# A post-norm attention and FP4 feed-forward layer on one core: a new order of work on four engines, a seeded value bias, a 17-matmul down projection

## The chip, the core and the metric

The kernel runs on one core of a Trainium2 chip. A core has TensorE (matmuls, PE in the profile; its weight loads are PEld), VectorE (DVE), ScalarE (ACT), GpSimd (POOL) and the SyncE queue (SP), each with its own program in order; they meet through semaphores. The metric is the device time of one execution in microseconds, the median of three runs.

## The reference, cut to what matters

The input is 16 sequences of 512 tokens of width 256. A linear attention with softmax features is followed by a residual and a layer norm, and then by a gated feed-forward layer (FFN) of hidden width 704 whose inputs and weights are rounded to FP4 in blocks of 16, again with residual and norm.

```python
q = features(x @ Wq + bq); k = features(x @ Wk + bk); v = x @ Wv + bv   # softmax over each head's 16
context = (q k^T / (sum(q) + eps)) v                                    # no softmax over tokens
x = layernorm(x + context @ Wo + bo)
gate = fp4(x) @ fp4(w_gate).T;  up = fp4(x) @ fp4(w_up).T
h = silu(gate) * up
x = layernorm(x + fp4(h) @ fp4(w_down).T)
```

## The kernel before

**Tiles and steps.** The 8192 tokens are NT = 64 tiles of 128 tokens, NS = 16 sequences of T = 4 tiles. `run` writes out, on every engine, a list of steps; step m of the attention works on tile m, and on older tiles with fixed lags. The FFN has steps of its own, 68 later (`JOIN = NS + 1` sequences), so that its tile 0 is begun in step 68; its preparations begin eight steps earlier. Nothing is scheduled at run time: the order written is the order run.

**Precision.** Every large product is made of three float32r products of a high and a low part (`three`, L859 in the profile): x_hi w_hi, x_hi w_lo, x_lo w_hi, for each of its chunks of 128 rows. ScalarE makes the high part (an `ACT.Copy`), VectorE or GpSimd the low part (a subtraction).

**An attention step on TensorE**: query and key (`pqk`, 6 matmuls of 512 columns), which add onto a bias that ScalarE has put into the bank (`seed`, L471); the value (`pv`): one matmul of `ones_r` with `bias_r` (L907) that opens the bank with the value bias in two pieces, then 6 of 256 columns; for tile m-2 the transposes of its features (L927) and the key-value sums (L929); the output projection of tile m-7 (`out_step`, 6 of 256 columns). Once in four steps there are the product of the sequence's sums with Wo (`pc`, L916), which needs VectorE's `kv_m`, and two transposes of one piece of FFN weights (L899). VectorE takes the maxima (L698), subtracts (L723), sums (L713) and inverts (L729), ScalarE takes the exponential (L533) and copies, GpSimd multiplies (`feat`, L374).

**The FFN weights** are 18 pieces of 128 rows (`NW`), one piece per sequence of attention steps, quantised by a chain over GpSimd, ScalarE and VectorE that ends with transposes, `wf_hi` (ScalarE, L548) and `wf_lo` (VectorE, L742). Pieces 17 and 18 fall into FFN steps 0 and 4; TensorE waits for the last one at FFN step 4.

**An FFN step on TensorE**: `gate_up(0)` (12 matmuls of 352 columns), transposes of the quantised hidden values of tile m-3 (`hq`, L970) and of the input of tile m+1 (L977), the down projection of tile m-4 (`three` over IC = 6 chunks: 18 matmuls of 256 columns), `gate_up(1)`. ScalarE runs Silu on the first half of tile m (L585) and the second half of tile m-1 (L571), the two steps of the rounding (L605, L610) and the high parts (L589, L594); VectorE multiplies (L824, L784), finds block maxima (L834, L793), inverts (L815) and makes low parts (L829, L840); GpSimd scales (`hxn`, L431), adds (`hc`, L416) and rescales (`hq`, L436). The last chunk of the hidden width holds 64 rows of data and 64 of zeros.

**Layer norms** take their statistics from ScalarE (`squares`, L492) and do 13 dependent small operations on VectorE (`layer_norm`, L641 to L655) for a batch of tiles at once. `LN_A` and `LN_B` give each batch's first tile, count, operations per step and first step; for the attention 24 and then 40 tiles, the second batch from attention step 72 on (FFN step 4).

## Time and profile before

| what | us |
|---|---|
| median of 3 runs | 745.06 (744.97 to 745.64) |
| the profiled execution's own time | 742.99 |
| its span, from the first to the last instruction | 741.3 |
| TensorE busy in the span | 705.2 |
| first attention tile's query and key until the last tile's | 8.28 to 252.95 |
| first `gate_up(0)` until the last tile's | 272.10 to 710.23 |

A row of a timeline gives the start and the length of an instruction, or of several merged, and in brackets how long the engine had been idle and what released it. Two successive starts give what an instruction costs when the engine is saturated; its length is longer, since matmuls overlap. A row of groups gives count, busy time, mean length, and idle time ahead of it. Windows give for each engine the busy time in a stretch and the mean granted clock as a share of 2.4 GHz.

### The profile page before, as it was taken

The page shows a single profiled execution, that of the slowest core. Times are in us where ns is not written, and L with a number is a line of the kernel's source. Part 1 is how long each engine was busy: PE and PEld are TensorE (multiplying, and loading weights), DVE is VectorE, ACT ScalarE, POOL GpSimd, SP SyncE. Part 2 cuts the span into 40 slices and gives each one's busy share as a digit, 9 for nine tenths or more (in the row PEclk, how much of TensorE's full clock was granted, in tenths as well). Part 3 has the DMA queues.
Part 4 walks back from the last instruction along what each step waited for, and adds up shares of the span by engine and source line. Part 5 has one row for each costly group of instructions (what it writes and reads, how often), then busy time and mean ns, then how long its engine had stood idle before and what let it go on. Part 6 is the DMA issues. An engine that isn't in the chain of part 4 may idle for free.

```text
span 741.3 us, 16606 instructions
## 1 busy us (share of the span) xinstructions
PE 705.2 (95%) x4908; PEld 674.0 (91%) x4908; DVE 619.4 (84%) x1517; ACT 551.1 (74%) x1227; POOL 558.8 (75%) x585
## 2 busy tenths in 40 slices
PE   7999999999999977799999999999999999999984
PEld 5899999888999867799999999999999999999984
DVE  5988999998999977799787787887899887898784
ACT  5677777777888775476777677677677788788777
POOL 4677777777777686687888788788788788787761
PEclk9999999999999999899999999999999999999998
DMA  5222222222222100000000000000000010111113
GB/s 162 60 79 79 72 80 79 66 79 83 68 80 79 43 23 1 1 2 1 1 2 1 2 1 1 2 2 1 1 1 2 15 45 29 44 44 36 53 65 135
DMA packets 40045, 30.04 MB, mean 41 GB/s; under 512 B 3474, under 2 KB 39956, under 8 KB 39956
## 3 DMA queue, kind: packets, MB, share of 16 engines
q1 hardware_dynamic: 37508, 26.75, 11.8%
q10 hardware_dynamic: 2448, 2.23, 1.1%
q8 instruction: 40, 0.66, 0.4%
q14 instruction: 49, 0.40, 0.2%
HBM read 20.58 MB, written 8.39 MB: 39 GB/s over the span
## 4 chain that ended last, share of the span: by engine, by line
PE 83%; issue 6%; DVE 4%; POOL 3%; ACT 2%; DMA 1%; SPq 0%; ACTq 0%; DVEq 0%; POOLq 0%
PE bank L859 63%; PE wide L859 6%; PE wide L970 5%; PE bank L929 3%; PE bank L927 2%; PE wide L916 2%; PE bank L977 2%; PE bank L907 1%; POOL scratch L388 1%; POOL scratch L374 1%; DMA scratch<-L_attn_Wv 1%; POOL scratch L431 1%; PE wide L899 0%; DVE scratch L847 0%; ACT scratch L497 0%
## 5 line engine op out<-in xcount | busy, mean ns | idle before, releaser
L859 PE MATMUL bank<-wf_hi,rounded 128*128 128x352 f32 (+1 forms) x1792 | 402.4, 309 | 12.5 <-DVE wf_lo L742 5.7
L859 PEld LDWEIGHTS bank<-wf_hi,rounded 128*128 128x128 f32 x1792 | 300.3, 190 | 15.6 <-DVE wf_lo L742 5.9
L859 PE MATMUL bank<-wf_lo,rounded 128*128 128x352 f32 (+1 forms) x896 | 273.8, 306 | 0.0
L859 PEld LDWEIGHTS bank<-wf_lo,rounded 128*128 128x128 f32 x896 | 170.3, 190 | 0.0
L431 POOL TENSOR_TENSOR scratch<-scratch 128x704 f32<-128x704 f32 x64 | 94.8, 1482 | 79.5 <-DVE scratch L815 75.9
L859 PE MATMUL bank<-qkv_hi,rounded 128*128 128x512 f32 (+1 forms) x512 | 147.4, 343 | 2.4 <-ACT bank L471 2.4
L416 POOL TENSOR_TENSOR scratch<-scratch 128x704 bf16<-128x704 f32 x64 | 99.4, 1553 | 8.5 <-ACT scratch L610 6.8
L859 PEld LDWEIGHTS bank<-qkv_hi,rounded 128*128 128x128 f32 x512 | 93.1, 191 | 13.2 <-issue 3.4
L380 POOL TENSOR_TENSOR rounded<-scratch,rounded 128x256 fp32r<-128x256 f32 x64 | 46.9, 734 | 58.8 <-ACT rounded L468 58.8
L605 ACT ACTIVATE scratch<-scratch 128x704 uint8<-128x704 f32 x64 | 50.6, 791 | 52.6 <-POOL scratch L431 51.6
L436 POOL TENSOR_TENSOR scratch<-scratch 128x704 f32<-128x704 bf16 x64 | 89.0, 1391 | 0.7 <-DVE scratch L819 0.7
L784 DVE TENSOR_TENSOR scratch<-scratch,bank 128x352 f32<-128x352 f32 x64 | 33.2, 519 | 67.4 <-ACT scratch L571 65.7
L859 PE MATMUL bank<-qkv_lo,rounded 128*128 128x512 f32 (+1 forms) x256 | 87.0, 340 | 0.0
L374 POOL TENSOR_TENSOR scratch<-scratch 128x512 f32<-128x512 f32 x64 | 68.0, 1063 | 10.6 <-DVE scratch L729 9.2
L492 ACT ACTIVATE dump<-res,row_sum 128x256 f32<-128x256 f32 x128 | 63.8, 498 | 1.4 <-DVE res L788 1.4
L829 DVE TENSOR_TENSOR rounded<-wide,rounded 128x768 fp32r<-128x768 f32 x64 | 61.0, 953 | 3.9 <-ACT rounded L589 3.4
L859 PE MATMUL wide<-rounded 128*128 128x256 f32 x384 | 60.6, 294 | 3.8 <-DVE rounded L749 2.2
L589 ACT ACTIVATE rounded<-wide 128x768 fp32r<-128x768 f32 x64 | 51.7, 808 | 10.0 <-PE wide L970 10.0
L859 PEld LDWEIGHTS wide<-rounded 128*128 128x128 f32 x384 | 51.2, 192 | 8.2 <-issue 5.9
L970 PE MATMUL wide<-ident,scratch 128*128 128x128 f32 x384 | 52.9, 274 | 2.7 <-POOL scratch L436 2.7
L585 ACT ACTIVATE scratch<-bank 128x352 f32<-128x352 f32 x64 | 29.4, 459 | 30.7 <-PE bank L859 30.5
L610 ACT ACTIVATE scratch<-scratch 128x704 bf16<-128x704 uint8 x64 | 50.6, 791 | 2.0
(102 smaller groups left out, 1505.5 us busy)
## 6 DMA issues: line engine op xcount, KB each, us to landing
scratch<-x_feat SPq DMA_DIRECT2D x64, 128.0 KB, 2.2
scratch<-x_tok SPq DMA_DIRECT2D x64, 128.0 KB, 2.1
out<-scratch SPq DMA_DIRECT2D x64, 128.0 KB, 1.7
scratch<-w_ffn ACTq DMA_DIRECT2D x17, 128.0 KB, 2.2
scratch<-L_attn_Wq SPq DMA_DIRECT2D x1, 256.0 KB, 3.3
scratch<-L_attn_Wk SPq DMA_DIRECT2D x1, 256.0 KB, 3.5
scratch<-L_attn_Wv SPq DMA_DIRECT2D x1, 256.0 KB, 4.9
wo<-L_attn_Wo SPq DMA_DIRECT2D x1, 256.0 KB, 4.1
```

Source lines behind the costliest of these rows:

```text
L374: pool.tensor_tensor(heads(feat[b]), prob[b][:, :, 0:HD], over(hrec[b], 2 * NH, HD), ALU.mult).then_inc(a_feat, 1)
L380: pool.tensor_tensor(xt_lo[s], xt_raw[s], xt_hi[s].bitcast(F32), ALU.subtract).then_inc(a_xlo, 1)
L416: pool.tensor_tensor(hc[b], hxn[b], hmg[b], ALU.add).then_inc(h_c, 1)
L431: pool.tensor_tensor(blocks(hxn[b1]), blocks(hid[b1]), over(binv[b1], NB), ALU.mult).then_inc(h_xn, 1)
L436: pool.tensor_tensor(hq[b][:, 0:I].rearrange("p (a c e) -> p a c e", a=11, e=BLK), hg[b].rearrange("p (a c e) -> p a c e", a=11, e=BLK), b ...
L492: act.activation(dump[:, :], res[:, rows(n)], ACT.Square, bias=row_sum[:, at], scale=-1.0 * D, accum_out=row_sq[:, at]).then_inc(sq, 1)
L589: act.activation(hqt_hi[b1][:, :, :], wide[:, 0:IP].rearrange("p (c n) -> p c n", c=IC), ACT.Copy).then_inc(h_hi, 1)
L605: act.activation(hy[b1], hxn[b1], ACT.Square, scale=BOWL).then_inc(h_y, 1)
L610: act.activation(hmg[b1], hy[b1], ACT.Copy, bias=FLOOR, scale=STEP).then_inc(h_mg, 1)
L829: dve.tensor_tensor(hqt_lo[b1][:, :, :], wide[:, 0:IP].rearrange("p (c n) -> p c n", c=IC), hqt_hi[b1][:, :, :].bitcast(F32), ALU.subtract ...
L859: last = pe.matmul(dst, x(c), w(c), start=first and n == 0, stop=n == len(terms) - 1, skip_group_check=not first)
L970: last = pe.transpose(wide[:, c * P:(c + 1) * P], hq[b1][:, c * P:(c + 1) * P], ident[:, :])
```

## The change

The steps are counted by tile rather than by sequence and tile, and every engine's step is written in a new order.

- The value bias is put into the bank by ScalarE (`v_seed`), as query and key's is, after it has copied the tile before out of the same bank; the matmul with `ones_r` and VectorE's three operations that prepared `bias_r` go.
- The down projection has 17 matmuls: in the sixth chunk w_lo stands in the weight rows that were zeros, and ScalarE writes a second copy of the 64 rows of `hqt_hi` beside the first (`h_dup`), so one matmul makes two of the three products. It takes tile m-5 instead of m-4 and stands first in the step.
- The weight pieces have their own steps (`PIECE_AT`): 12 at every fourth step, then 6 at every third; the last is begun at step 62 and transposed at 67. TensorE waits for all 18 at FFN step 0. One small VectorE operation of each piece (`w_sc`) goes.
- The FFN's tile 0 is begun at step 67 rather than 68. On TensorE, the features of tile m-3 rather than m-2 come first in an attention step, the value product last.
- The first norm's batches are 32 and 32 tiles, from steps 44 and 82 (FFN step 15); the squares of the later 32 tiles go at three in two steps from step 61 (`SQUARE_AT`).
- ScalarE takes the Silu of the second half (L591) in the tile's own step rather than in the next.

```diff
+PIECE_AT = tuple(range(0, 48, 4)) + tuple(range(47, 65, 3))
+PIECE_G, PIECE_T = 3, 5
 LN_SLOTS = {1: (4,), 2: (1, 5), 3: (0, 3, 6), 4: (0, 2, 4, 6), 7: (0, 1, 2, 3, 4, 5, 6)}
-LN_A = ((0, 24, 1, 32), (24, 40, 2, 72))
+LN_A = ((0, 32, 1, 44), (32, 32, 2, 82))
+SQUARE_AT = tuple(range(9, 41)) + tuple(61 + k * 2 // 3 for k in range(32))
...
-        A_FROM, A_LOOP, A_TO = -1, (4, NS - 1), NS + 14
+        A_FROM, A_TO = -1, NS + 16
         B_FROM, B_TO = -2, NS + 3
-        JOIN = NS + 1
+        JOIN = NT + 3
 
...
-            for i in range(A_FROM, JOIN + B_TO):
-                for t in range(T):
-                    if i < A_TO:
-                        attention(i, [t])
-                    if i - JOIN >= B_FROM:
-                        ffn(i - JOIN, [t])
-
-        def w_bank(i):
-
-            return pkv if isinstance(i, int) and i > NS else pc
+            for m in range(T * A_FROM, JOIN + T * B_TO):
+                if m < T * A_TO:
+                    attention(m)
+                if m - JOIN >= T * B_FROM:
+                    ffn(m - JOIN)
 
         def rows(m):
...
+            def v_seed(n):
+                need(act, a_v, n)
+                act.activation(pv[:, 0:D], bias_b[:, 2 * D:3 * D], ACT.Copy).then_inc(a_vseed, 1)
...
+                for n in tile(m):
+                    need(act, a_qkv, n + 1)
+                    need(act, a_post, n - 1)
+                    act.activation(v_sb[n % 2], pv[:, 0:D], ACT.Copy).then_inc(a_v, 1)
+                for n in tile(m + 1):
+                    if n > 0:
+                        v_seed(n)
...
+                for n in tile(m - 1):
+                    need(act, h_xn, n + 1)
+                    need(act, h_mg, n - 1)
+                    act.activation(hy[n % 2], hxn[n % 2], ACT.Square, scale=BOWL).then_inc(h_y, 1)
+                for n in tile(m):
+                    need(act, gu_b, n + 1)
+                    need(act, h_b, n)
+                    act.activation(gated[1], pg[1][:, 0:HALF], ACT.Silu, scale=SHY ** -2).then_inc(si_b, 1)
+                for n in tile(m - 1):
+                    need(act, h_y, n + 1)
+                    need(act, h_c, n - 1)
+                    need(act, h_g, n - 1)
+                    act.activation(hmg[n % 2], hy[n % 2], ACT.Copy, bias=FLOOR, scale=STEP).then_inc(h_mg, 1)
+                for n in tile(m - 3):
+                    need(act, h_lo, n + 1)
+                    act.activation(hqt_hi[n % 2][TAIL:P, IC - 1, :], wide[0:TAIL, (IC - 1) * P:IP],
...
+                    if j < NW - KC:
+                        dve.tensor_tensor(wf_lo[:, :, piece], pc[:, 0:D].rearrange("p (c n) -> p c n", c=KC),
+                                          wf_hi[:, :, piece].bitcast(F32), ALU.subtract).then_inc(w_los, 1)
+                    else:
+                        dve.tensor_tensor(wf_lo[:, 0, piece], pc[:, 0:P], wf_hi[:, 0, piece].bitcast(F32), ALU.subtract)
+                        dve.tensor_tensor(wf_hi[TAIL:P, 1, piece], pc[TAIL:P, P:D],
+                                          wf_hi[TAIL:P, 1, piece].bitcast(F32), ALU.subtract).then_inc(w_los, 1)
+                for n in tile(m - 7):
...
+            pe.matmul(pv[:, 0:D], ident[:, :], mask[:, :, :], start=True, stop=True).then_inc(opened, 1)
...
-                        pe.matmul(pv[:, 0:D], ones_r[:, :], bias_r[:, :], start=True, stop=False,
-                                  skip_group_check=True)
-                        qkv(pv[:, 0:D], t, 2 * D, 3 * D).then_inc(a_qkv, 1)
...
+            def query_key(n):
+                need(pe, a_xlo, n + 1)
+                need(pe, a_seed, n + 1)
+                qkv(pqk[n % 2][:, :], n % T, 0, 2 * D).then_inc(a_qk, 1)
+
+            def attention(m):
+                for n in tile(m - 3):
+                    b = n % 2
+                    need(pe, a_feat, n + 1)
+                    need(pe, a_v, n + 1)
+                    need(pe, a_qlo, n - 1)
+                    if n % T == 0:
+                        need(pe, a_kvm, n // T)
+                    for c in range(KC):
+                        pe.transpose(pqt[b][:, c * P:(c + 1) * P], feat[b][:, c * P:(c + 1) * P], ident[:, :])
+                    for c in range(KC):
+                        last = pe.matmul(pkv[:, c * P:(c + 1) * P], v_sb[b][:, c * P:(c + 1) * P],
+                                         feat[b][:, D + c * P:D + (c + 1) * P],
+                                         start=n % T == 0 and c == 0, stop=n % T == T - 1, skip_group_check=True)
+                    last.then_inc(a_post, 1)
+                if m % T == T - 1:
+                    for n in tile(m):
+                        query_key(n)
+                for j in pieces(m - PIECE_T):
+                    need(pe, w_qs, j + 1)
+                    need(pe, w_los, j)
+                    need(pe, a_clo, min((m - 3) // T, NS))
+                    for c in range(KC):
+                        last = pe.transpose(pc[:, c * P:(c + 1) * P], w_q[:, c * P:(c + 1) * P], ident[:, :])
+                    last.then_inc(w_t, 1)
+                for n in tile(m - 7):
+                    need(pe, a_qlo, n + 1)
+                    need(pe, a_clo, n // T + 1)
+                    need(pe, a_res, n)
+                    three(po[:, 0:D], lambda c: qt_hi[n % T][:, c, :], lambda c: qt_lo[n % T][:, c, :],
+                          lambda c: c_hi[:, c, :], lambda c: c_lo[:, c, :], KC).then_inc(a_out, 1)
+                if m % T != T - 1:
+                    for n in tile(m):
+                        query_key(n)
+                for q in seqs(m - 6):
+                    if q == 0:
+                        pe.wait_ge(ld_wo, 32)
+                    need(pe, a_kvm, q + 1)
+                    need(pe, w_los, sum(at + PIECE_T <= m for at in PIECE_AT))
+                    for c in range(KC):
+                        last = pe.matmul(pc[:, c * D:(c + 1) * D], kv_m[:, c, :], wo[:, c, :],
+                                         start=True, stop=True)
+                    last.then_inc(a_c, 1)
+                for n in tile(m):
+                    if n == 0:
+                        pe.wait_ge(wq_lo_s, 3)
+                    need(pe, a_vseed, n + 1)
+                    qkv(pv[:, 0:D], n % T, 2 * D, 3 * D).then_inc(a_qkv, 1)
 
             def gate_up(h, b):
                 for dst, at in ((pg[h], 0), (pu[h], IP)):
@@ -942,49 +899,47 @@
 
...
-                    if isinstance(i, int) and (i, t) == (1, 0):
-                        pe.wait_ge(w_los, NW)
...
+                if m == 0:
+                    pe.wait_ge(a_sub, NT)
+                    pe.wait_ge(a_v, NT)
+                    pe.wait_ge(w_los, NW)
+                if m == 3:
+                    pe.wait_ge(a_res, NT)
+                    pe.wait_ge(a_clo, NS)
+                    pe.wait_ge(consts, 7)
+                for n in tile(m - 5):
+                    b = n % 2
+                    need(pe, h_lo, n + 1)
+                    need(pe, y_s, n)
+                    three(pd[:, 0:D], lambda c: hqt_hi[b][:, c, :], lambda c: hqt_lo[b][:, c, :],
+                          down(wf_hi), down(wf_lo), IC - 1, last=False)
+                    pe.matmul(pd[:, 0:D], hqt_lo[b][:, IC - 1, :], down(wf_hi)(IC - 1), start=False, stop=False)
+                    need(pe, h_dup, n + 1)
+                    pe.matmul(pd[:, 0:D], hqt_hi[b][:, IC - 1, :], down(wf_hi)(IC - 1),
+                              start=False, stop=True).then_inc(d_s, 1)
+                for n in tile(m):
+                    need(pe, x_lo, n + 1)
+                    need(pe, h_a, n)
+                    gate_up(0, n % 2).then_inc(gu_a, 1)
+                for n in tile(m + 1):
+                    need(pe, x_q, n + 1)
+                    need(pe, x_lo, n)
+                    for c in range(KC):
+                        last = pe.transpose(pxt[:, c * P:(c + 1) * P],
+                                            xq[:, n % T * D + c * P:n % T * D + (c + 1) * P], ident[:, :])
+                    last.then_inc(x_t, 1)
+                for n in tile(m - 3):
+                    need(pe, h_q, n + 1)
+                    need(pe, h_dup, n)
+                    for c in range(IC):
+                        last = pe.transpose(wide[:, c * P:(c + 1) * P], hq[n % 2][:, c * P:(c + 1) * P], ident[:, :])
+                    last.then_inc(h_t, 1)
+                for n in tile(m):
+                    need(pe, h_b, n)
+                    gate_up(1, n % 2).then_inc(gu_b, 1)
 
             run(pe, attention, ffn)
 
```

Where TensorE goes from the attention to the FFN, it had these rows ahead of the first `gate_up` (L927, L929: features and sums; `wide<-rounded`: an output projection; L916: product with Wo; L977: first input transpose; L899: a weight piece's transpose):

```order
L927 MATMUL bank<-ident,scratch 128x128 x2
L929 MATMUL bank<-scratch 128x128 x2
L859 MATMUL wide<-rounded 128x256 x6
L927 MATMUL bank<-ident,scratch 128x128 x2
L929 MATMUL bank<-scratch 128x128 x2
L859 MATMUL wide<-rounded 128x256 x6
L916 MATMUL wide<-wo,scratch 128x256 x2
L859 MATMUL wide<-rounded 128x256 x6
L977 MATMUL bank<-ident,scratch 128x128 x2
L859 MATMUL wide<-rounded 128x256 x6
L899 MATMUL bank<-ident,scratch 128x128 x2
L859 MATMUL bank<-wf_hi,rounded 128x352
```

and has these now (L851, L853, L882, L931 and L865 are the same in the new numbering):

```order
L851 MATMUL bank<-ident,scratch 128x128 x2
L853 MATMUL bank<-scratch 128x128 x2
L820 MATMUL wide<-rounded 128x256 x6
L851 MATMUL bank<-ident,scratch 128x128 x2
L853 MATMUL bank<-scratch 128x128 x2
L820 MATMUL wide<-rounded 128x256 x6
L882 MATMUL wide<-wo,scratch 128x256 x2
L931 MATMUL bank<-ident,scratch 128x128 x2
L865 MATMUL wide<-ident,scratch 128x128 x2
L820 MATMUL wide<-rounded 128x256 x6
L820 MATMUL bank<-wf_hi,rounded 128x352
L820 MATMUL bank<-wf_lo,rounded 128x352
```

Two output projections stood between the product with Wo and the first `gate_up`, now one does; the last weight piece's transposes are ahead of it too.

In an FFN step TensorE had, from the end of `gate_up(0)` on (L970 hidden, L977 input transposes, then the down projection):

```order
L859 MATMUL bank<-wf_lo,rounded 128x352
L859 MATMUL bank<-wf_hi,rounded 128x352 x2
L859 MATMUL bank<-wf_lo,rounded 128x352
L859 MATMUL bank<-wf_hi,rounded 128x352
L970 MATMUL wide<-ident,scratch 128x128 x6
L977 MATMUL bank<-ident,scratch 128x128 x2
L859 MATMUL bank<-wf_hi,rounded 128x256
L859 MATMUL bank<-wf_lo,rounded 128x256
L859 MATMUL bank<-wf_hi,rounded 128x256 x2
```

and has now, from the end of the down projection on (L919 and L921 are its last two matmuls) to the transposes behind `gate_up(0)`:

```order
L919 MATMUL bank<-wf_hi,rounded 128x256
L921 MATMUL bank<-wf_hi,rounded 128x256
L820 MATMUL bank<-wf_hi,rounded 128x352
L820 MATMUL bank<-wf_lo,rounded 128x352
L820 MATMUL bank<-wf_hi,rounded 128x352 x2
L820 MATMUL bank<-wf_lo,rounded 128x352
L820 MATMUL bank<-wf_hi,rounded 128x352 x2
L820 MATMUL bank<-wf_lo,rounded 128x352
L820 MATMUL bank<-wf_hi,rounded 128x352 x2
L820 MATMUL bank<-wf_lo,rounded 128x352
L820 MATMUL bank<-wf_hi,rounded 128x352
L931 MATMUL bank<-ident,scratch 128x128 x2
```

The down projection stands ahead of both halves instead of between them, and ends in two single matmuls instead of three of a chunk.

On VectorE the last piece's `wf_lo` (L742) stood behind an FFN step's work and two operations of the second norm batch (L641, L645; `rounded<-wide` is `hqt_lo`):

```order
L829 TENSOR_TENSOR rounded<-wide,rounded 128x768
L834 TENSOR_REDUCE scratch<-scratch 128x22
L840 TENSOR_TENSOR rounded<-bank,rounded 128x256
L847 TENSOR_TENSOR scratch<-scratch 128x512
L641 TENSOR_SCALAR ln_v<-row_sq 128x40
L645 TENSOR_SCALAR ln_h<-ln_v 128x40
L742 TENSOR_TENSOR wf_lo<-bank,wf_hi 128x2x128
L779 TENSOR_REDUCE scratch<-res 128x32
```

and stands now (L661, L662) ahead of the first FFN tile's products, right behind the preparations (L773 maxima, L783 `xqt_lo`, L798 the rounding's sum):

```order
L773 TENSOR_REDUCE scratch<-res 128x32
L783 TENSOR_TENSOR rounded<-bank,rounded 128x256
L789 RECIPROCAL scratch<-scratch 128x32
L798 TENSOR_TENSOR scratch<-scratch 128x512
L661 TENSOR_TENSOR wf_lo<-wide,wf_hi 128x128
L662 TENSOR_TENSOR wf_hi<-wide,wf_hi 64x128
L667 SCALAR_TENSOR_TENSOR res,row_sum<-wide,scratch 128x256
```

It has moved from the fifth FFN step to the first, and no norm operation stands near it.

## Rows read from the trace of the kernel before

**Rows 1.** The first part of the page: busy us (share) xinstructions of each engine.
```profile
PE 705.2 (95%) x4908; PEld 674.0 (91%) x4908; DVE 619.4 (84%) x1517; ACT 551.1 (74%) x1227; POOL 558.8 (75%) x585
```

**Rows 2.** Six stretches end to end: engines' busy us, PE clock, DMA.
```profile
core 0: us, PE busy (x) PEld busy (x) DVE busy (x) ACT busy (x) POOL busy (x), PEclk, DMA share, GB/s
...
8.28:252.95 244.67, 242.41 (x1611) 219.34 (x1612) 221.02 (x561) 186.44 (x493) 177.52 (x228) 1.00 0.27 77
252.95:272.10 19.15, 13.01 (x81) 11.02 (x79) 16.07 (x46) 13.20 (x36) 14.14 (x20) 0.91 0.12 36
272.10:310.03 37.93, 29.27 (x175) 27.72 (x176) 27.28 (x60) 22.38 (x47) 25.83 (x27) 0.91 0.00 0
310.03:710.23 400.20, 398.40 (x2901) 396.07 (x2901) 335.43 (x786) 302.29 (x598) 326.37 (x285) 1.00 0.04 14
710.23:741.30 31.07, 18.30 (x140) 17.27 (x138) 18.29 (x64) 23.15 (x50) 11.12 (x8) 0.91 0.31 107
```

**Rows 3.** TensorE in order of time, attention tile and two W products: start, us.
```profile
92.97 0.28 PE L907 MATMUL bank<-bias_r,ones_r 128*128 128x256 f32 x1
93.08 0.28 PE L859 MATMUL bank<-qkv_hi,rounded 128*128 128x256 f32 x1
...
93.80 0.60 PE L916 MATMUL wide<-wo,scratch 128*128 128x256 f32 x2
...
109.39 1.03 PE L916 MATMUL wide<-wo,scratch 128*128 128x256 f32 x4
```

**Rows 4.** Chain that ended last, steady FFN tiles: start, us, line.
```profile
342.66 5.97 PE bank L859 x42
...
541.21 5.97 PE bank L859 x42
```

**Rows 5.** TensorE in order of time, down projection, then end of last gate_up.
```profile
713.28 0.28 PE L859 MATMUL bank<-wf_lo,rounded 128*128 128x256 f32 x1
713.40 0.40 PE L859 MATMUL bank<-wf_hi,rounded 128*128 128x256 f32 x2
...
716.71 0.32 PE L859 MATMUL bank<-wf_hi,rounded 128*128 128x352 f32 x1
716.87 0.82 PE L970 MATMUL wide<-ident,scratch 128*128 128x128 f32 x6
```

**Rows 6.** TensorE between the stages, with waits in brackets: idle before, releaser.
```profile
260.77 0.44 PE L927 MATMUL bank<-ident,scratch 128*128 128x128 f32 x2 [2.42 <-POOL scratch L374]
...
268.79 0.95 PE L859 MATMUL wide<-rounded 128*128 128x256 f32 x6 [2.19 <-DVE rounded L749]
...
272.10 0.40 PE L859 MATMUL bank<-wf_hi,rounded 128*128 128x352 f32 x1 [0.16 <-DVE rounded L840]
...
300.91 0.66 PE L859 MATMUL bank<-wf_hi,rounded 128*128 128x352 f32 x1 [5.66 <-DVE wf_lo L742]
```

**Rows 7.** VectorE in order of time, around the last weight piece.
```profile
299.08 1.44 DVE L645 TENSOR_SCALAR ln_h<-ln_v 128x40 uint32<-128x40 uint32 x1
300.44 0.41 DVE L742 TENSOR_TENSOR wf_lo<-bank,wf_hi 128x256 fp32r<-128x256 f32 x1
```

**Rows 8.** Groups by line and shape, attention stretch: busy, mean ns | idle.
```profile
L514 ACT ACTIVATE scratch<-bank 128x256 f32<-128x256 f32 x62 | 23.3, 376 | 17.1 <-PE bank L929 13.6 <-PE bank L859 3.0
...
L707 DVE TENSOR_SCALAR scratch<-scratch 128x16 f32<-128x16 f32 x16 | 9.5, 592 | 0.0
...
L703 DVE TENSOR_SCALAR scratch<-scratch 128x16 f32<-128x16 f32 x16 | 2.9, 181 | 0.0
```

**Rows 9.** ScalarE in order of time, at the first Silu.
```profile
274.14 1.28 ACT L585 ACT_TABLE_LOAD   x1
```

**Rows 10.** TensorE in order of time, the drain: start, us, idle before.
```profile
726.75 0.87 PE L970 MATMUL wide<-ident,scratch 128*128 128x128 f32 x6 [1.04 <-POOL scratch L436]
...
730.66 0.35 PE L859 MATMUL bank<-wf_hi,rounded 128*128 128x256 f32 x1 [0.88 <-DVE res L788]
```

**Rows 11.** ScalarE in order of time, the last outputs.
```profile
736.95 2.07 ACT L497 ACTIVATE scratch<-res,nbias,rstd 128x256 f32<-128x256 f32 x4 [1.27 <-DVE nbias L649]
```

897 lines of the change are left out of this document (367 added, 530 removed).

## The prediction, before the changed kernel was run

> **What bounds the kernel now.** The page gives TensorE 705.2 of 741.3 us busy [rows 1], a share that hides four different stretches, so I cut the span at TensorE's own landmarks [rows 2]. They add up to it: 8.28 (where the first row shown begins) until the first query and key, 244.67 of attention, 19.15 until the first `gate_up`, 37.93 for the first five FFN steps, 400.20 for 58 more, 31.07 from the last `gate_up(0)` on. In the attention and in the 58 steps TensorE is busy 242.41 of 244.67 and 398.40 of 400.20, while the others have room: VectorE 221.02 and 335.43, ScalarE 186.44 and 302.29, GpSimd 177.52 and 326.37. There, a matmul taken out is time taken out. Between them TensorE is idle for 6.1 us (19.15 less 13.01) and 8.7 us (37.93 less 29.27), and in the last stretch for 12.8 us: there the order of work sets the time.
>
> What a matmul costs is read from starts, not lengths. The bias matmul starts at 92.97, its successor at 93.08 [rows 3]; in the down projection one start follows another after 0.12 us, 713.28 to 713.40 [rows 5]. I take 0.118 for a 256-column matmul. One of 352 takes 0.16, 716.71 to 716.87 [rows 5]. A sequence of four tiles takes 15.59 us, from one product with Wo at 93.80 to the next at 109.39 [rows 3]. An FFN step takes 6.847: 342.66 to 541.21 is 29 steps [rows 4]; 24 x 0.16 and 18 x 0.118 of it leave 0.88 for 8 transposes, 0.11 each.
>
> **The change, part by part.** Each term is against the profiled execution's stretches.
>
> *Value bias.* 63 of the 64 matmuls lie between the landmarks: 63 x 0.118 = 7.4 us less. ScalarE gets one 256-column copy per tile. Its nearest row is 376 ns [rows 8], 23.7 us over 63 tiles, which raises it from 186 to 210 of some 237: covered by TensorE's matmuls, as long as it comes in time. On the step's clock: the features and sums, which free `v_sb`, are first and take at most 1 us (two transposes, two products of 128 columns); then come the copy of the last value and the seed, two copies of 0.38, so the seed is in by 1.8. The value product is last, 6 x 0.118 = 0.7 of a step of (15.59 - 0.47) / 4 = 3.78, and starts at about 3.0. Slack 1.2 us. Queued behind that copy are the high parts, the exponential and the next seed for query and key, which have a step or more to spare. VectorE loses `w_sc`, 592 ns a piece [rows 8], but works pieces closer together from step 47 on.
>
> *A busier end of the attention.* From step 57 ScalarE normalises a tile per step, from 61 it squares three in two steps, and pieces come every third. It has 186.44 / 63 = 2.96 us per tile today; with the seed's 0.38, a normalising of 0.52 (four in 2.07 [rows 11]) and half a square, some 0.3, it needs 4.2 in a step of 3.8, for three steps: 1 us lost, at most 4. With the first steps roughly even, the last tile's query and key start at 252.95 - 7.4 + 0.5 = 246 (bounds 245 and 250).
>
> *To the first gate_up.* TensorE's own 13.0 us there lose one output projection (0.72) and little else, so 12 is the floor and today's 19.15 the ceiling. The two large waits are for GpSimd's features, 2.42, and for `c_lo`, 2.19 [rows 6]. The features of the last tiles no longer stand behind so much FFN preparation, and starting the FFN a step earlier takes one projection out of the way; but the chain maxima, subtract, exponential, sum, invert, features, sums, `kv_m`, product with Wo, `c_hi`, `c_lo` stays, and now the last weight piece must get through it too, since the first `gate_up` waits for all 18. Walking the new order with today's durations gives about 15; I take 15.5.
>
> *First five FFN steps.* Their matmuls are 3 steps of two gates and the input transposes (24 x 0.16 + 0.22 = 4.06), one with the hidden transposes (4.72), one with the down projection as well (6.84), and the leftovers, two output projections and two pieces' transposes (12 x 0.118 + 4 x 0.11 = 1.86): 25.6 against 37.93. The largest hole is 5.66 us for the last `wf_lo` [rows 6]; VectorE had it behind norm operations, the last of 1.44 us, and started it at 300.44 [rows 7]. The new order has none there. What stays: 1.28 us of table load before the first Silu [rows 9] and pipelines that fill. The clock is at 0.91 of 2.4 GHz over the stretch [rows 2], that is, at the 1.2 GHz level for part of it; TensorE had idled before. The new content is 25.8 (an output projection more, two pieces' transposes fewer; the down projection comes at the front of the sixth step and is counted here). With 4 us of waits and half clock I take 30, between 26 and 35.
>
> *58 steps.* Each loses a matmul: 6.847 - 0.118 = 6.729, times 58 is 390.3. The stretch has 3.1 us over 58 x 6.847 = 397.1 today, when norm operations delay VectorE. The second norm batch of the attention moves in here, but has 32 columns and not 40; I keep 3: 393.3. Cover: VectorE has 5.74 us of work per tile (335.43 over 58.45 steps), GpSimd 5.58 and ScalarE 5.17, plus 0.38 at most for `h_dup`, all below 6.73. `h_dup` waits for `h_lo` and TensorE's next hidden transposes wait for it; I put it at 2 us into the next step, the transposes at 17 x 0.118 + 12 x 0.16 + 0.22 = 4.1. Its other reader is the down projection two steps on.
>
> *The drain.* The last gates ended 6.64 after `gate_up(0)` began (710.23 to 716.87 [rows 5]), now 2.1 less, since the down projection between them has moved to the front and one more of them is left for afterwards, where TensorE waits anyway: 1.04 ahead of the last hidden transposes, 0.88 ahead of the last down projection [rows 10]. Silu of the second half now stands ahead of the rounding of the tile before, which starts GpSimd perhaps 0.6 later; the matmul saved gives 0.1 back. From the last norm's results on, 4.35 us of outputs stay [rows 11]. 31.07 becomes 29.2 (29.0 to 31.1).
>
> Sum: 246 + 15.5 + 30 + 393.3 + 29.2 = 714.0 us of span, 27.3 less than 741.3. The profiled execution took 742.99, 1.7 more than its span, and the median of the runs, 745.06, is 2.1 above that: **717.8 us**.
>
> **Rules weighed.** TensorE starts 256-column matmuls 0.118 us apart [rows 5]. By the Trainium skill ("TensorE: Matmul & The Clock Gate", Back-to-back issue gap) an isolated matmul of N columns at full clock takes N/2.4 + 2.5 ns, 109 ns here; the trace differs by a tenth. By that rule the 127 matmuls would give 13.8 us instead of 15.0, and the sum would be 719.
>
> The same VectorE operation on 16 columns took 181 ns in one place of the order and 592 in another [rows 8], and the norm's operations on 40 took 1.44 where GpSimd worked [rows 7]. The Trainium skill ("SBUF — State Buffer", Who interferes with whom) has it that the two share a port pair, that whoever comes first keeps it for its instruction, and the other stands still. By that rule a new order can make VectorE slower with the same work, which is the second rival's mechanism.
>
> **The rivals.**
> 1. *The stage change stays as long* (chance 0.17). The chain of features to `c_lo` sets it, not the order: the waits of 2.42 and 2.19 speak for that. Then 19.2 and 35 stand in the sum for 15.5 and 30: 726.5.
> 2. *The FFN step is no longer TensorE's* (0.14). VectorE's operations fall on GpSimd's, or the loop ScalarE, VectorE, GpSimd (`hmg`, `hc`, `hxn`, then `hq`) comes out at 6.85 to 7.0. GpSimd's 5.58 of 6.73 speaks against it; for it, that every second step carries the preparation of a pair of tiles, and is fuller than the mean. 58 x 0.2 = 12: about 729.5.
> 3. *Slower* (0.06). There is a single value bank: product, copy, seed, product is a loop through two engines. If ScalarE comes to the pair only behind exponential, seed, high part and squares, the value product waits in every step. It decides from 0.43 us per step: 27.3 / 64. The seed must then come 3.4 us into the step instead of 1.8. At 0.6 per step, 756. ScalarE's 76% in the attention speaks against it.
> 4. *No change* within 0.2% (0.02), by gains and losses that cancel.
> 5. *Better still* (0.03): stage change at 13 and 27, and no excess in the 58 steps: 705.
>
> **How the numbers follow.** The forecast holds 0.58, with 711 to 725 as its own range: the terms' bounds seldom all fall on one side. The range 709 to 732 takes in it, the first two rivals nearly whole, and leaves out some 0.16. Within 0.2% is about what this kernel's measurement can tell from no change. Faster: 0.58 + 0.17 + 0.14 + 0.03 = 0.92; same 0.02; slower 0.06.
>
> **What the new profile would show.** Right: a sequence at 15.1 us between products with Wo; no wait of TensorE for the value seed; FFN gates 6.73 apart; no wait of several us for `wf_lo`; first `gate_up(0)` near 261 to 262, the sixth near 291, the last near 685, 29 us before the end. Wrong: value products that wait for ScalarE in most steps (rival 3); gates 6.85 or more apart with TensorE waiting for VectorE or `h_dup` (rival 2); more than 18 us between the last query and key and the first gate (rival 1).

## The result and the profile after

The changed kernel takes **708.02 us** (median; 707.44 to 708.51), the kernel before 745.01 (743.12 to 745.64): ratio **0.9504**, 95% interval 0.9492 to 0.9517. Forecast were 717.8 us and a range from 709 to 732, so the sign is right and the time lies a microsecond below the range: the gain is 37.0 us, where 27.3 were forecast.

The head of the page of after, where [rows 1] stand for before:

```profile
span 705.7 us, 16440 instructions
PE 681.2 (97%) x4782; PEld 656.9 (93%) x4782; DVE 627.4 (89%) x1498; ACT 577.1 (82%) x1355; POOL 562.0 (80%) x581
PEclk9999999999999999999999999999999999999999
```

The same six stretches as [rows 2], cut at the same landmarks in after:

```profile
0.00:9.40 9.40, 3.98 (x11) 2.96 (x11) 1.38 (x2) 3.61 (x6) 3.03 (x16) 0.99 0.66 183
9.40:241.73 232.33, 231.52 (x1551) 212.76 (x1551) 208.52 (x550) 194.37 (x513) 179.54 (x234) 0.99 0.29 82
241.73:257.72 15.99, 10.63 (x73) 8.92 (x71) 15.39 (x41) 14.73 (x42) 14.11 (x19) 1.00 0.08 25
257.72:285.17 27.45, 26.58 (x177) 26.01 (x178) 22.66 (x51) 20.67 (x48) 21.03 (x21) 1.00 0.00 1
285.17:675.79 390.62, 390.62 (x2845) 389.47 (x2844) 362.72 (x798) 320.19 (x700) 333.39 (x287) 1.00 0.04 15
675.79:705.70 29.91, 17.92 (x135) 16.76 (x133) 16.73 (x59) 23.47 (x51) 10.91 (x8) 0.94 0.32 111
```

Put beside the prediction's terms:

| stretch, us | before | forecast | after | error |
|---|---|---|---|---|
| until the last query and key | 252.95 | 246 | 241.73 | -4.3 |
| to the first gate_up | 19.15 | 15.5 | 15.99 | +0.5 |
| five FFN steps | 37.93 | 30 | 27.45 | -2.6 |
| 58 FFN steps | 400.20 | 393.3 | 390.62 | -2.7 |
| last gates to the end | 31.07 | 29.2 | 29.91 | +0.7 |
| span | 741.3 | 714.0 | 705.7 | -8.3 |

The other 1.5 of the 9.8 us lie outside the span: from span to median I allowed 3.8 us, and it is 2.3. Of the 3.8, 2.1 were the distance of one profiled execution from the median of its kernel, which had no reason to come again; here it is 0.6.

In the fifth row TensorE is busy for all of its 390.62 us, 58 x 6.735: no step is longer than its matmuls. VectorE is busy for 362.72 us there, 93%, where before had 335.43 in 400.20 for the same 58 tiles. TensorE's waits from shortly before the last query and key to the third FFN step, which answer to [rows 6] (us in total, times, longest):

```profile
PE bank L851 <- POOL scratch L376: 2.8, 2, 1.4
PE bank L820 <- DVE wf_hi L662: 1.3, 1, 1.3
PE bank L931 <- POOL scratch L399: 1.0, 1, 1.0
PE bank L820 <- DVE res L667: 0.9, 1, 0.9
```

The wait of 5.66 for `wf_lo` is gone, and the granted clock is 1.00 over both middle stretches, where before had 0.91 in each. A step of the attention in after, as ScalarE and TensorE show it (rows of other engines left out): the value's copy (L540), the seed (L453) and the value product.

```profile
106.18 0.37 ACT L540 ACTIVATE scratch<-bank 128x256 f32<-128x256 f32 x1
...
106.59 0.39 ACT L453 ACTIVATE bank<-bias_b 128x256 f32<-128x256 f32 x1
...
107.86 0.28 PE L820 MATMUL bank<-qkv_hi,rounded 128*128 128x256 f32 x1
```

The seed ends at 106.98, the value product starts at 107.86: 0.88 us of slack where I had walked to 1.2, and TensorE nowhere waits for L453. Rival 3 had no ground. The costs of the new and the slowed operations, by groups:

```profile
L453 ACT ACTIVATE bank<-bias_b 128x256 f32<-128x256 f32 x64 | 24.9, 388 | 2.0
...
L599 ACT ACTIVATE rounded<-wide 64x128 fp32r<-64x128 f32 x64 | 17.3, 270 | 11.6 <-DVE rounded L802 10.4
```

```profile
L794 DVE TENSOR_TENSOR scratch<-scratch 128x704 bf16<-128x704 bf16 x64 | 58.4, 913 | 2.6 <-POOL scratch L405 2.6
```

### The profile page after: what moved, and what is told of

Its sections match the earlier page's. It is cut to its first block, busy times and chain, and to the rows that moved or that the text cites. A ratio compares the mean times of both kernels' runs of the same rounds, so it can differ in the third digit from the quotient of the medians.

```text
span 705.7 us, 16440 instructions
## 1 busy us (share of the span) xinstructions
PE 681.2 (97%) x4782; PEld 656.9 (93%) x4782; DVE 627.4 (89%) x1498; ACT 577.1 (82%) x1355; POOL 562.0 (80%) x581
## 4 chain that ended last, share of the span: by engine, by line
PE 88%; ACT 4%; DVE 3%; issue 3%; DMA 1%; POOL 1%; ACTq 0%; SPq 0%; DVEq 0%; POOLq 0%
PE bank L820 66%; PE wide L938 6%; PE wide L820 5%; PE bank L853 4%; PE bank L931 2%; PE bank L851 2%; PE wide L882 2%; PE bank L921 1%; PE bank L919 1%; DMA bias_b<-L_attn_bk 1%; ACT scratch L480 1%; PE wide L865 0%; ACT dump L475 0%; ACT res L480 0%; ACT bank L449 0%
## 5 line engine op out<-in xcount | busy, mean ns | idle before, releaser
L820 PE MATMUL bank<-wf_hi,rounded 128*128 128x352 f32 (+1 forms) x1664 | 387.0, 310 | 4.0 <-DVE res L768 1.7
L820 PEld LDWEIGHTS bank<-wf_hi,rounded 128*128 128x128 f32 x1664 | 283.9, 189 | 5.2 <-issue 3.9
L820 PE MATMUL bank<-wf_lo,rounded 128*128 128x352 f32 (+1 forms) x832 | 255.2, 307 | 0.0
L820 PEld LDWEIGHTS bank<-wf_lo,rounded 128*128 128x128 f32 x832 | 157.6, 189 | 0.0
L416 POOL TENSOR_TENSOR scratch<-scratch 128x704 f32<-128x704 bf16 x64 | 94.9, 1482 | 38.9 <-DVE scratch L794 38.9
L411 POOL TENSOR_TENSOR scratch<-scratch 128x704 f32<-128x704 f32 x64 | 89.3, 1395 | 3.7 <-DVE scratch L765 3.7
L475 ACT ACTIVATE dump<-res,row_sum 128x256 f32<-128x256 f32 x128 | 64.5, 504 | 0.9 <-DVE res L768 0.6
L802 DVE TENSOR_TENSOR rounded<-wide,rounded 128x768 fp32r<-128x768 f32 x64 | 60.6, 946 | 1.6 <-ACT rounded L575 1.6
L794 DVE TENSOR_TENSOR scratch<-scratch 128x704 bf16<-128x704 bf16 x64 | 58.4, 913 | 2.6 <-POOL scratch L405 2.6
L399 POOL TENSOR_TENSOR scratch<-scratch 128x256 f32<-128x256 bf16 x64 | 39.8, 622 | 20.2 <-DVE scratch L746 17.9
L820 PEld LDWEIGHTS bank<-qkv_lo,rounded 128*128 128x128 f32 x256 | 48.9, 191 | 4.6
```

The source lines that it names most:

```text
L411: pool.tensor_tensor(blocks(hxn[n % 2]), blocks(hid[n % 2]), over(binv[n % 2], NB), ALU.mult).then_inc(h_xn, 1)
L416: pool.tensor_tensor(hq[n % 2][:, 0:I].rearrange("p (a c e) -> p a c e", a=11, e=BLK), hg[n % 2].rearrange("p (a c e) -> p a c e", a=11, e ...
L475: act.activation(dump[norm][:, :], res[:, rows(n)], ACT.Square, bias=row_sum[:, at], scale=-1.0 * D, accum_out=row_sq[:, at]).then_inc(sq, 1)
L794: dve.tensor_tensor(hg[n % 2], hc[n % 2], hmg[n % 2], ALU.subtract).then_inc(h_g, 1)
L802: dve.tensor_tensor(hqt_lo[n % 2][:, :, :], wide[:, 0:IP].rearrange("p (c n) -> p c n", c=IC), hqt_hi[n % 2][:, :, :].bitcast(F32), ALU.su ...
L820: op = pe.matmul(dst, x(c), w(c), start=first and n == 0, stop=last and n == len(terms) - 1, skip_group_check=not first)
```

## The experiments

Eighteen kernels. To compare them across chips, "against after" is the difference of their ratios to before, times 745; "slower" and "faster" mean that the interval of the ratio leaves out 1, even where the distance is under 2%. The stretches are those of the profiled execution, cut at the landmarks above (attention from the first to the last query and key; five: from the first to the sixth `gate_up(0)`).

| run | median | ratio | attention | to gate | five | 58 steps | end |
|---|---|---|---|---|---|---|---|
| before | 745.01 | 1 | 244.67 | 19.15 | 37.93 | 400.20 | 31.07 |
| after | 708.02 | 0.9504 | 232.33 | 15.99 | 27.45 | 390.62 | 29.91 |
| e1 | 712.81 | 0.9582 | 231.65 | 15.48 | 29.04 | 397.58 | 29.25 |
| e2 | 714.56 | 0.9613 | 239.60 | 15.84 | 27.37 | 390.53 | 29.90 |
| e3 | 750.52 | 1.0093 | 246.04 | 19.15 | 37.65 | 402.87 | 34.07 |
| e4 | 708.07 | 0.9515 | 232.59 | 15.75 | 30.00 | 390.62 | 29.90 |
| e5 | 752.35 | 1.0093 | 245.77 | 20.49 | 37.31 | 402.91 | 34.30 |
| e6 | 744.44 | 0.9996 | 245.90 | 18.89 | 37.14 | 400.23 | 31.05 |
| e7 | 725.52 | 0.9743 | 231.33 | 15.99 | 33.26 | 403.39 | 30.94 |
| e8 | 726.88 | 0.9749 | 231.31 | 15.98 | 33.29 | 401.61 | 31.14 |
| e9 | 1052.18 | 1.4138 | 232.08 | 15.98 | 34.08 | 713.63 | 41.82 |
| e10 | 708.58 | 0.9516 | 232.68 | 17.35 | 27.36 | 390.53 | 29.90 |
| e11 | 706.19 | 0.9480 | 232.29 | 14.54 | 27.39 | 390.61 | 29.91 |
| e12 | 817.75 | 1.0974 | 231.95 | 15.98 | 31.53 | 492.76 | 33.36 |
| e13 | 753.67 | 1.0120 | 244.65 | 19.30 | 36.53 | 409.41 | 31.86 |
| e14 | 754.99 | 1.0134 | 246.86 | 19.33 | 36.77 | 405.95 | 34.68 |
| e15 | 749.43 | 1.0061 | 250.72 | 18.67 | 37.27 | 400.21 | 31.02 |
| e16 | 744.51 | 0.9996 | 245.74 | 20.21 | 37.03 | 398.03 | 33.28 |
| e17 | 739.67 | 0.9932 | 231.61 | 16.32 | 31.85 | 418.03 | 29.91 |
| e18 | 705.55 | 0.9471 | 232.02 | 14.54 | 27.43 | 390.62 | 29.90 |

### What the two matmuls are worth, in either order: e1, e2, e3, e5, e6

**e1**: after, with 18 matmuls.

```diff
-                          down(wf_hi), down(wf_lo), IC - 1, last=False)
-                    pe.matmul(pd[:, 0:D], hqt_lo[b][:, IC - 1, :], down(wf_hi)(IC - 1), start=False, stop=False)
-                    need(pe, h_dup, n + 1)
-                    pe.matmul(pd[:, 0:D], hqt_hi[b][:, IC - 1, :], down(wf_hi)(IC - 1),
-                              start=False, stop=True).then_inc(d_s, 1)
+                          down(wf_hi), down(wf_lo), IC).then_inc(d_s, 1)
```

> The kernel after with the down projection back to 18 matmuls: the last six weight pieces are rounded into high and low parts over all 128 rows, the copy h_dup is gone. My theory: in the 58 steps TensorE is the bound, so a 256-column matmul costs its 0.118 us in each of 64 tiles: 708.0 + 7.55 = 715.6 us, FFN gates 6.85 apart, with no excess in any step. Rival: h_dup, which reads the bank that the hidden transposes write next, costs something that the shorter projection hides; then the gates come out under 6.85 and the time at 711 to 714.

Measured 0.9582 (0.956 to 0.9605), 5.8 us against after. The 58 steps grew from 390.62 to 397.58, 0.120 each: the term of the forecast. The gates are 6.85 apart, so the rival falls, though the median lies among its times. The total came out under the 7.55 of my theory: the attention and the end were 0.7 shorter each in the profiled execution, for no reason of the edit that I know.

**e2**: after, with the bias by a matmul of ones.

```diff
-                    need(pe, a_vseed, n + 1)
+                    need(pe, a_v, n)
+                    pe.matmul(pv[:, 0:D], ones_r[:, :], bias_r[:, :], start=True, stop=False,
+                              skip_group_check=True)
```

> The kernel after with the value bias again as a matmul of ones by the rounded bias, ahead of the value product, and without the seed copy. Theory A: the matmul costs 0.118 us per tile, and the other 0.03 of the 0.147 by which a tile became shorter comes from the order: 715.5 us, a sequence at 15.47. Theory B: all of the 0.147 is the matmul's (it has another kind of weights and of input than its neighbours): 717.4 us, a sequence at 15.59. Rival on the other side: the seed copy on ScalarE held something up, so that its removal pays part back: below 713.

Measured 0.9613 (0.9591 to 0.9634), 8.1 us against after; the attention 232.33 to 239.60, 7.27 or 0.115 per tile. The starts of query and key in a steady sequence are 15.47 us apart (after 15.00, before 15.59). Theory A, to the hundredth: the matmul is 0.118, and 0.12 us per sequence come from the order.

**e3**: before, with both matmuls gone and its own order. **e5** and **e6**: each alone. Their main lines, on ScalarE:

```diff
+                    if live(i, t, -3):
+                        need(act, h_lo, m - 2)
+                        act.activation(hqt_hi[b1][TAIL:P, IC - 1, :], wide[0:TAIL, (IC - 1) * P:IP],
+                                       ACT.Copy).then_inc(h_dup, 1)
...
                         act.activation(v_sb[b1], pv[:, 0:D], ACT.Copy).then_inc(a_v, 1)
+                        if live(i, t):
+                            v_seed(m)
```

> The kernel before, in its old order, with the seeded value bank and the down projection in 17 matmuls, nothing else. If the matmuls' worth is the same in either order, 745.0 - 64 x (0.118 + 0.118) = 729.9 us, which leaves 21.9 of the 37.0 us to the order of work. Rival: the old order has no room for the seed between the copy of the last value and the value product, or for h_dup between the low part and the next hidden transposes; then TensorE waits in each tile and less than 10 us are gained, 735 us or more.

> The kernel before with the down projection in 17 matmuls and h_dup, nothing else. In e3 every second FFN step took 7.08 us and not 6.73, and the chain of waits went through ScalarE, VectorE and GpSimd (second Silu, product, residual, maxima, hxn, hy, hmg, h_dup, and round). My theory: h_dup lengthens that loop past TensorE's 6.73, so this kernel alone shows 7.08 and 6.73 in turn and is 3 to 6 us slower than before. Rival: the loop of e3 came from the seed's displacement of other work; then it gains 7 us.

> The kernel before with the seeded value bank, nothing else. In e3 a sequence took 15.66 us, 0.07 more than before, though a matmul of 0.118 was taken out of each tile; TensorE waited in the output projections instead. My theory: the seed's copy moves the high and low parts of the query back in ScalarE's and VectorE's order, so the attention does not get shorter: a sequence at 15.6 to 15.7, and 0 to 3 us slower than before (the broadcast load of bv at the start among it). Rival: a sequence at 15.12, 7 us faster, and the waits of e3 came from something else.

This is where the reasoning broke. With a matmul less in each of 64 tiles, in either stage, e3 is **slower** than before, 1.0093 (1.0075 to 1.0112). The seed alone gives 0.9996 (0.9984 to 1.0009): nothing. The shorter projection alone costs 1.0093 (1.0064 to 1.0122), 7 us. In e3 and e5 FFN steps take 7.08 and 6.73 us in turn. The chain of e3 through one such step (start us, us, engine, line; L583 is the second half's Silu, L798 its product, L802 the residual, L807 and L819 maxima and scale, L829 reciprocal, L431 `hxn`, L617 `hy`, L625 `h_dup`; pieces left out are marked, among them 0.60 us of an output, L504, in the second step):

```profile
439.75 0.27 ACT rounded L625
...
440.55 0.45 ACT scratch L583
...
441.46 0.15 DVE res L802
...
441.89 0.43 DVE scratch L807
...
442.49 0.63 DVE scratch L819
...
443.26 0.44 DVE scratch L829
...
443.86 1.47 POOL scratch L431
...
445.35 0.80 ACT scratch L617
...
446.99 0.27 ACT rounded L625
...
453.55 0.08 ACT rounded L625
```

There is no row of TensorE in it. From one `h_dup` to the next it is 7.24 us, then 6.56: 13.80 for two steps, which TensorE would do in 13.46. Without the two `h_dup` the two rounds come to 13.26 by my estimate, 13.80 less twice 0.27, just under the 13.69 of two steps before. In the attention of e6 a sequence takes 15.66 us though each tile has a matmul less; TensorE now stops ahead of the output projections (four sequences of e6):

```profile
PE wide L859 <- issue: 1.1, 3, 0.4
PE wide L859 <- DVE res L677: 0.3, 1, 0.3
```

### Where the excess went: e4, e7, e8, e17

**e4**: after, with the norm's batches of before. `LN_A = ((0, 24, 1, 33), (24, 40, 2, 73))`, `SQUARE_AT = tuple(range(9, 73))`.

> The kernel after with the first norm in batches of 24 and 40 tiles, started at steps 33 and 73, and a square per step, as before (a step later). Theory A: the batches' place and size took the excess away; then it comes back: some 0.45 us in each of three sequences from step 33 on and about 1.1 in two FFN steps, 1.4 + 2.3 = 3.7 us, 711.7. Theory B: the new order on VectorE absorbs the norm operations wherever they stand: 708.0 to 708.8.

Measured 0.9515 (0.9494 to 0.9536): 0.8 us against after, within the interval. The sequences are 15.0 and the 58 steps 390.62 as before the edit; only the last seven tiles took 0.6 more, and kernels that are the same there differ by as much. Theory B: in the new order it costs nothing where the batches stand. The 2.5 us more in "five" are the clock, below.

**e7**: after, with the second half's Silu back at the front of the next step.

```diff
             def ffn(m):
...
+                for n in tile(m - 1):
+                    need(act, gu_b, n + 1)
+                    need(act, h_b, n)
+                    act.activation(gated[1], pg[1][:, 0:HALF], ACT.Silu, scale=SHY ** -2).then_inc(si_b, 1)
                 for g, n in ready(m, LN_B):
...
-                for n in tile(m):
-                    need(act, gu_b, n + 1)
-                    need(act, h_b, n)
-                    act.activation(gated[1], pg[1][:, 0:HALF], ACT.Silu, scale=SHY ** -2).then_inc(si_b, 1)
```

> The kernel after with one lag undone: the Silu of a tile's second half stands again at the front of the next step on ScalarE, behind hmg and h_dup of the tile before. It starts about 1.4 us later. Walked with the durations of after, the round of Silu, product, maxima, scales, hxn, hy, hmg, h_dup and Silu is then about 6.8 us in steps with a norm's normalising, against TensorE's 6.73. Theory A: the early Silu is what freed the FFN steps: gates 6.8 to 6.95, 3 to 12 us slower than after. Theory B: it is slack now, and the other changes of order freed the steps: within 1.5 us of after, mostly in the last stretch.

> As e7, and VectorE's residual of the FFN again between the product of the second half and its maxima, as before, which puts 0.44 us more into the same round. Theory A: a round of 7.1 to 7.3 us, at least in every second step: gates at 6.9 or more on average, 10 to 25 us slower than after and close to e3's FFN. Theory B: still slack somewhere (GpSimd's hc and hq are in another order): less than 3 us.

e7: 0.9743 (0.9723 to 0.9762), **17.8 us** against after, more than theory A's bound. Every second of the FFN steps 6 to 14 takes 7.95. VectorE has no norm operation there; what these steps have and others lack are two squares of the first norm on ScalarE (L475), ahead of the moved Silu; the last of them fall into step 14. The steps with that norm's operations on VectorE (15 to 21) take 6.7 to 7.1, as plain ones do, and three of those with the second norm's first batch 7.75. What TensorE waits for in the 58 steps is the product behind the moved Silu:

```profile
PE bank L820 <- DVE scratch L750: 7.3, 9, 1.0
```

e8, with the residual early as well (the block of L766 moved ahead of L752): 0.9749 (0.9721 to 0.9777), the same as e7. The numbers of its theory A came (18.3 us against after, steps of 6.92 on average), but not by its cause: e7 has them without the residual, whose place costs nothing beside the Silu's.

**e17**: after, with `x_lo` at the end of VectorE's step (the block of L780 to L784 moved behind L808).

> The kernel after with one operation of VectorE moved: x_lo, the low part of the next tile's input, at the end of its step, behind hg, h_lo and the last maxima, as before. It then ends about when TensorE comes to the gates that need it (in after the last maxima end 0.3 us ahead of them). Theory A: this place is the second thing that keeps the norm's operations off TensorE's path: 0.1 to 0.3 us in every step and about a microsecond in those with norm operations, 12 to 30 us slower than after. Theory B: the early Silu is enough in the new order: less than 3 us slower.

0.9932 (0.9912 to 0.9951), 32 us against after: nearly the whole gain of the change is gone by one VectorE operation in another place. Every second step takes 7.55 us, the others 6.85, and the wait is the one expected (L807 is `x_lo` there):

```profile
PE bank L820 <- DVE rounded L807: 19.5, 28, 1.0
```

### The two places put into the old order: e13, e14, e16

**e13**: before, with the Silu of `m` between `hy` and `hmg`. **e14**: the same on e5. **e16**: e14 with the input's transposes, `x_hi` and `x_lo` ahead of the hidden tile's parts.

```diff
-                    if live(i, t, -1):
-                        need(act, gu_b, m)
-                        need(act, h_b, m - 1)
-                        act.activation(gated[1], pg[1][:, 0:HALF], ACT.Silu).then_inc(si_b, 1)
...
+                    if live(i, t):
+                        need(act, gu_b, m + 1)
+                        need(act, h_b, m)
+                        act.activation(gated[1], pg[1][:, 0:HALF], ACT.Silu).then_inc(si_b, 1)
```

> The kernel before with one thing moved: the second half's Silu of a tile stands in its own step on ScalarE, between hy and hmg, as in after, and not at the front of the next step. Theory A: the late Silu is what turned norm operations into excess; the 58 steps then come down from 400.2 to 397.5 to 398.5 us and the first five from 37.9 by 1 to 3: 2 to 5 us faster than before. Theory B: in the old order something else holds the round (the residual ahead of the maxima, hy and hmg behind three other copies): within 1 us of before, or slower, since the Silu now holds up hmg, which waits behind it.

> e5 (the kernel before with 17 matmuls, 7 us slower than before) and the early Silu of e13. Theory A: the early Silu alone gives the matmul its worth in the old order: gates 6.73 apart in steps without norm operations, 58 steps at 391 to 394 us, 7 to 12 us faster than before and 14 to 19 faster than e5. Theory B: the early Silu is not enough: every second step at 6.9 or more, less than 4 us faster than before.

> e14 (the kernel before with 17 matmuls and the early Silu, 10 us slower than before) and the next tile's input moved ahead of the hidden tile's parts on three engines, as in after: TensorE transposes it ahead of hidden, ScalarE copies x_hi ahead of hqt_hi, VectorE subtracts x_lo right behind the first half's product. Theory A: with the Silu early, x_lo at the end of VectorE's step, behind the norm's operations, is what TensorE waits for in steps with norm operations (7.6 to 8.7 us in e13 and e14); the 58 steps come down from 405.9 to 391 to 393.5 us, some 13 us faster than e14 and 2 to 6 us faster than before. Theory B: the norm's operations hold up another link (product, scales, hg) all the same: 58 steps at 398 or more.

e13: 1.0120 (1.0098 to 1.0143), slower, so its theory A falls. e14: 1.0134 (1.0117 to 1.0151); its theory A was half right. In plain steps of e14 the gates are 6.73 to 6.78 apart, not 7.08 and 6.73 as in e5, so the early Silu does give the missing matmul its worth. But the steps with norm operations went up to 8.7 us. VectorE of e13 ahead of one late gate (start us, us; L651 is a norm operation on 32 columns, L840 is `x_lo`):

```profile
549.06 1.18 DVE L647 TENSOR_SCALAR rstd<-ln_h 128x32 int32<-128x32 uint32 x1
...
553.49 0.51 DVE L834 TENSOR_REDUCE scratch<-scratch 128x22 f32<-128x352 f32 x1
553.92 1.01 DVE L651 SCALAR_TENSOR_TENSOR ln_t<-rstd 128x32 f32<-128x32 f32 x1
554.85 0.41 DVE L840 TENSOR_TENSOR rounded<-bank,rounded 128x256 fp32r<-128x256 f32 x1
```

and what TensorE waits for in the steps of e13:

```profile
PE bank L859 <- DVE rounded L840: 5.7, 7, 1.1
```

`x_lo` ends at 555.26, the gates start at 555.32. e16 takes that away: 0.9996 (0.9981 to 1.0011), 10 us faster than e14; plain steps 6.73, the steps of 8.7 still there, later norm steps 7.83 once in two, 58 steps at 398.03. That is theory B's number (398 or more) and not A's 391 to 393.5: the input first removes part of the excess, but TensorE still waits for a residual of VectorE (6.3 us in six waits) in steps with norm operations. What else of the order frees those was not tried one by one.

### The same question in the attention: e15

e6, with ScalarE's copy of the query ahead of the value's copy and its seed.

```diff
+                    if t < 3 and live(i, t, -3):
+                        q_hi()
                     if live(i, t, -1):
                         need(act, a_qkv, m)
...
-                    if t < 3 and live(i, t, -3):
-                        q_hi()
```

> e6 (the kernel before with the seeded value bank, no faster than before) with ScalarE's copy of the query's high part ahead of the value's copy and its seed, not behind them, in three tiles of four. Theory A: in e6 TensorE waited in the output projections for the query's low part, which the seed had pushed back; now it does not, and a sequence takes 15.1 to 15.3 us instead of 15.66: 5 to 8 us faster than before. Theory B: the value's seed is late instead and TensorE waits ahead of the value product: a sequence at 15.5 or more, within 2 us of before.

1.0061 (1.0046 to 1.0076), a sequence at 16.1 us. Theory A falls. TensorE's weight loads now wait for the seed itself (L474), as theory B has it, and it costs more than B allowed:

```profile
PEld bank L859 <- ACT bank L474: 2.9, 8, 0.5
```

My reading of e6 and e15 together: ScalarE of the old order has two copies that TensorE wants early, and whichever is second is late. Which of the new order's moves opens that place is not shown.

### Lags and the stage change: e9, e12, e10, e11, e18

**e9**: after, with the down projection of `m - 4` at the front of TensorE's step. **e12**: with VectorE's residual at `m - 4` as well.

```diff
-                for n in tile(m - 5):
+                for n in tile(m - 4):
                     b = n % 2
                     need(pe, h_lo, n + 1)
```

> The kernel after with the other lag undone: the down projection of tile m - 4 instead of m - 5 at the front of TensorE's step. Its h_lo then ends about when the step begins (VectorE writes it some 0.9 us before the last maxima of its step) and h_dup about 0.5 us later. My theory: TensorE waits for h_lo at the front of each step, 0.3 to 1.2 us: 20 to 70 us slower than after; that is, the lag of five was needed to move the projection to the front. Rival: the projection starts when it did, and only the run-in and the drain change: within 1 us of after, perhaps a us faster, since the last projection stands a step earlier.

> The kernel after with the down projection of tile m - 4 at the front of TensorE's step, and VectorE's residual of tile m - 4 too. (In e9 the residual stayed at m - 5, behind the product that needs the Silu after the step's last gates, so that TensorE waited for the whole round with each projection; that run says what one projection bank costs when only one engine is moved, not what the lag is worth.) Theory A: in after h_lo of the step's tile ends 1.3 us behind the start of the next step's projection; the round projection, first gates, Silu, product, x_lo, hg, h_lo is 7.5 to 8.0 us, so the gates stand that far apart: 50 to 80 us slower than after. Theory B: VectorE's h_lo comes early once TensorE is late, the round closes at 6.73, and only start and end differ: within 2 us of after.

e9 takes 1052 us, far outside both theories, by a wait I had not walked: TensorE in its 58 steps

```profile
PE bank L820 <- DVE res L768: 227.3, 57, 5.6
```

The residual of `m - 5` frees the one projection bank, and it stands behind the product that needs the Silu of the last gates, those of the step before: a round through the whole step. e12, with both engines moved, takes 817.75 us, 1.0974 (1.0947 to 1.1), 110 against after and more than theory A's 50 to 80, with the wait that A named (L802 is `h_lo`):

```profile
PE bank L820 <- DVE rounded L802: 66.2, 55, 2.3
```

With the rest of the new order as it is, the projection at the front needs the lag of five.

**e10**: `JOIN = NT + 4`. **e11**: bq and bk loaded ahead of Wk, and the wait for weight pieces split; **e18**: the split alone.

```diff
                     pe.wait_ge(a_v, NT)
-                    pe.wait_ge(w_los, NW)
+                    pe.wait_ge(w_los, 2 * IC)
                 if m == 3:
                     pe.wait_ge(a_res, NT)
                     pe.wait_ge(a_clo, NS)
+                    pe.wait_ge(w_los, NW)
```

> The kernel after with the FFN's steps laid one later over the attention's (JOIN = NT + 4). In the prediction the step earlier was worth part of 19.15 - 15.5 us. Theory A: the chain of the last features to c_lo and the last weight piece sets the first gate, so that it starts where it did and only its waits become shorter: within 1 us of after. Theory B: the first gate comes later by the attention work of a step, one output projection of 0.72 and what it waits for, 1.5 to 3 us slower; then the step was worth that much.

> The kernel after with two small changes in different stretches: the loads of the biases bq and bk ahead of Wk's, since the first seed waited 2.79 us for bk in after, and TensorE's wait for all 18 weight pieces split into 12 (the gates' own) ahead of the first gate and 18 ahead of the first hidden transposes. Theory: the first query and key at 8.0 us or earlier instead of 9.40 (it lay between 8.46 and 9.58 in four kernels with the same start), and the first gate 0.8 to 1.3 us sooner after the last query and key than 15.99: about 2 us faster than after. Rival: the first gate then waits for the low part of its input instead and nothing is gained there; the landing of Wk, a us later, takes the place of bk's.

> The kernel after with TensorE's wait for all 18 weight pieces split alone, without the reordered loads of e11. In e11 the first gate came 14.54 us after the last query and key, not 15.99. Theory: 1.45 us faster than after, and as fast as e11, whose loads gained nothing (the first query and key began at 9.71). Rival: the hidden transposes then wait as long for the last piece, so that nothing is left of it at the sixth gate.

e10: 0.9516 (0.9497 to 0.9534), 0.9 us against after, which is within theory A's 1 us and within the interval; but the first gate came 1.36 later, near theory B's 1.5. By the stretches the step earlier is worth 1.4 us of the 3.2. e11: 0.9480 (0.9466 to 0.9494); e18: **0.9471** (0.9457 to 0.9485), 2.5 us faster than after with intervals that do not touch. The windows of e18, in the columns of [rows 2]:

```profile
241.41:255.95 14.54, 10.52 (x72) 8.92 (x71) 13.97 (x37) 13.31 (x38) 12.70 (x18) 1.00 0.10 28
255.95:283.38 27.43, 26.56 (x178) 26.10 (x178) 24.05 (x55) 22.17 (x52) 22.42 (x22) 1.00 0.01 1
```

1.45 us come from the first gate, which no longer waits for the last down-projection piece, and the five steps behind stay as they were. The rest of the 2.5 is within what these runs spread. The reordered loads gained nothing: in e11 Wk landed late in bk's place. e18 is the fastest version here.

## Why the prediction was right, and where it was wrong

**The step that failed.** The prediction put the new order at nothing in the two stretches where TensorE is busy: it took 7.4 us of matmuls out of the attention and no more, and kept before's excess in the 58 steps ("I keep 3"). The runs show 5.07 us for the order in the attention (e2 against before) and an excess of 0.3 (390.62 against 58 x 6.729 = 390.3). The rest of the miss of 9.8 is a term for waits and half clock in the five steps that was 2.6 too long, and 1.5 between span and median; a first product that came 1.1 later, and two small terms of 0.5 and 0.7, went the other way.

**The two matmuls** (7.4 and 6.8 us): right in the new order, by e1 and e2 (0.120 and 0.115 us each). But the prediction took this as their worth in any order and the order as an addition to it. e3, e5 and e6 show that they are no sum: in the old order they are worth nothing or -7 us. The order is what turns them into time.

**The attention** (246, measured 241.73). e2, which has the 64 bias matmuls back, is still 5.07 us below before in this stretch. By the starts of query and key that is 1.7 in the first eight tiles, 1.4 in the three sequences that the first norm batch made 0.47 longer before (now 0.0), 1.6 of 0.12 in each of the 13 later ones, and some 0.4 spread over others. Which move of the order gave which part was not tried. The "busier end" is not what failed: after lost about 1.2 us over its steady pace in the last four sequences, near the 1 us walked. It was not ScalarE's share that cost most, though: 0.7 of it lies in one tile, where TensorE waited for the low part of a weight piece (L658):

```profile
PE wide L882 <- DVE wf_lo L658: 0.5, 1, 0.5
```

The sum of the prediction took in only 0.5 of that 1 us. The first query and key came 1.1 later in after. One profiled execution of each kernel shows 8.43 to 9.58 with after's order and loads, 8.28 to 9.75 with before's loads (e5, e13, e14, e16), and 8.95 to 10.20 in e3, e6 and e15, which have before's order and the broadcast load of bv. The ranges lie over one another, so nothing here speaks for a cost of that load.

**To the first gate** (15.5, measured 15.99): right; features and last piece were the waits named. e10 and e18 size two parts, 1.4 for the earlier step and 1.45 still in it for the last piece. Rival 1 fell.

**Five FFN steps** (30, measured 27.45): the content of 25.8 leaves 1.65 for waits, where I had 4 for waits and half clock. The clock did not fall in after. It can: the first FFN step of after, and of e4, with the same instructions of TensorE (in e7, whose TensorE did the same work up to there too, it took 6.48 at 0.74):

```profile
257.72:262.69 4.97, 4.97 (x33) 4.78 (x33) 2.04 (x6) 3.04 (x7) 3.10 (x6) 1.00 0.01 3
```

```profile
256.82:264.53 7.71, 7.71 (x33) 7.65 (x33) 2.41 (x6) 3.05 (x6) 3.08 (x6) 0.60 0.01 2
```

That is 2.74 us for the same work, and e4's stretch came out at the forecast's 30.0. The other three executions of e4 had spans 0.4 to 1.9 us shorter than this one: I take the fall for chance between executions, which no second trace of one kernel shows. The forecast should have carried it as a branch and not as a mean.

**58 steps** (393.3, measured 390.62): 6.729 per step was right, "I keep 3" was wrong. I had put the 3.1 us of excess down to how much the norm adds to VectorE, and so kept it when the work stayed. VectorE is busy for 27 us more than before (362.72 against 335.43) and yet no step is longer. e4 shows that it is not the batches' place. e7 and e17 show two places that the new order cannot do without, the second half's Silu and `x_lo`, on whose results TensorE's next gates wait: moved back alone they cost 18 and 32 us. They are short and now stand ahead of what can be late. They are not all of it: e16, the old order with both moved to where after has them, keeps 7.7 us of excess (398.03 against 390.3). Rival 2 was the right mechanism with the wrong verdict: the round is real, by the estimate at e3 it was near the step's length in the kernel before, and the new order opened it.

**The drain** (29.2, measured 29.91): inside its bounds; what fills the 0.7 was not tried.

**The range** ended at 709 because it took the excess and the attention's norm sequences as costs that could only stay or grow. Rival 5 is near where the time came out, but by luck: its own terms (13 and 27 for 15.5 and 30, and 3 less in the 58 steps) give 717.8 - 8.5 = 709.3 and not the 705 written there, the stage change took 15.99 and not 13, and it has nothing for the attention, where most was gained.

## What to carry to other kernels

A matmul taken out is time taken out only while the round through the other engines is shorter than the step: measure that round (follow the chain from an operation to the same one a step later) before summing, and when the order of work changes too, give it a term of its own. Where a step has slack in every engine and still comes out long, look for the short operation that TensorE waits for behind long ones, and ask of each lag which single bank or buffer its reader frees. A wait for "all pieces" ahead of a loop that needs two thirds of them at first is worth splitting.

## What the runs showed of the hardware

The VectorE operation on 704 bf16 columns (`hg`) took 913 ns on average in after and 488 before (L794 and L819). In a step of after it starts while GpSimd's `hxn` (L411) runs, in one of e9 GpSimd is idle until it is done:

```profile
443.41 1.40 POOL L411 TENSOR_TENSOR scratch<-scratch 128x704 f32<-128x704 f32 x1
...
443.91 1.28 DVE L794 TENSOR_TENSOR scratch<-scratch 128x704 bf16<-128x704 bf16 x1
```

```profile
506.20 0.51 DVE L794 TENSOR_TENSOR scratch<-scratch 128x704 bf16<-128x704 bf16 x1
...
506.86 1.39 POOL L416 TENSOR_TENSOR scratch<-scratch 128x704 f32<-128x704 bf16 x1 [6.26 <-DVE scratch L794]
```

The Trainium skill ("SBUF — State Buffer", Who interferes with whom) has the two engines share a port pair under an exclusive lock, and a VectorE instruction with two inputs in SBUF contend with a GpSimd instruction that reads SBUF. These rows agree, 1.28 us beside 0.51, and the slowed one ended 0.38 us after `hxn` did. In the 58 steps `hg` takes 54.4 us in after and 28.4 in before; VectorE's whole busy time there grew by 27, other operations having risen and fallen. The new order collides more here than the old one, and it costs no time: TensorE has no wait in those 58 steps.

After 5.0 to 5.4 us of idle time in the stretch ahead, TensorE's granted clock in the first FFN step was 1.00 in after, e2 and e8, 0.75 in e1, 0.74 in e7 and 0.60 in e4: up to 2.7 us between executions of nearly the same program. In e12 TensorE idles 2.3 us ahead of every second step. Two such steps, each with one wait of 2.3 us for `h_lo`:

```profile
442.00:452.76 10.76, 8.50 (x51) 8.20 (x50) 7.72 (x16) 5.14 (x11) 7.84 (x7) 0.84 0.01 2
460.01:469.27 9.26, 7.00 (x52) 6.69 (x51) 7.48 (x16) 5.14 (x11) 6.37 (x6) 1.00 0.00 0
```

The one in which the granted clock fell (0.84 on average) took 1.50 us more for the same work, so there a wait costs more than its length.
